# Attention with the pass for the maxima of all 64 items in front of the second pass

## The reference

```python
q = x @ Wq.T + bq; k = x @ Wk.T + bk; v = x @ Wv.T + bv   # then heads, a rotary factor
k = jnp.repeat(k, rep, axis=1); v = jnp.repeat(v, rep, axis=1)
att = jnp.einsum('bhqd,bhkd->bhqk', q, k) / scale
att = jnp.where(causal[None, None], att, -jnp.inf)
att = jax.nn.softmax(att, axis=-1)
y = jnp.einsum('bhqt,bhtd->bhqd', att, v)
return y.transpose(0, 2, 1, 3).reshape(b, t, n) @ Wo.T + bo
```

## Time and profile before

| | us |
|---|---|
| median of 3 runs | 3045.74 |
| lowest and highest | 3042.68, 3046.11 |
| profiled execution | 3042.04 |
| its span | 3040.3 |
| second block of attention, first to last product | 156.09 to 315.8 |
| first product of the third block | 317.40 |

### The profile page before, as it was taken

One profiled execution on the slowest core, in us unless ns is written; L12 is line 12 of the kernel. 1 busy time (PEld: TensorE's weight loads), 2 busy tenths in 40 slices (PEclk: granted clock), 3 DMA queues, 4 the chain that ended last, 5 costly groups with the idle time before them and its releaser, 6 DMA issues. The chain is left out here.

```text
span 3040.3 us, 79963 instructions
## 1 busy us (share of the span) xinstructions
PE 2766.1 (91%) x33106; PEld 2176.6 (72%) x33106; DVE 1597.8 (53%) x3536; ACT 1285.3 (42%) x2840; POOL 469.5 (15%) x603
## 2 busy tenths in 40 slices
PE   7899888999928999999999999999999999699998
PEld 4433557999815777777777777777777778589997
DVE  4444447666424554555555555555554554476763
ACT  1123212223114555655555565556555555332321
POOL 0011000000001222222222222222222322100000
PEclk9979899999958999999999999999999999899999
DMA  1100011111010000000000000000000000111100
GB/s 43 29 1 1 22 49 56 56 35 48 0 28 23 20 16 12 20 23 5 23 20 16 13 20 23 6 23 20 16 12 20 23 6 6 30 56 55 55 28 14
DMA packets 62021, 73.90 MB, mean 24 GB/s; under 512 B 17152, under 2 KB 51344, under 8 KB 61712
## 3 DMA queue, kind: packets, MB, share of 16 engines
q1 hardware_dynamic: 61712, 69.44, 7.5%
HBM read 68.25 MB, written 1.18 MB: 23 GB/s over the span
## 5 line engine op out<-in xcount | busy, mean ns | idle before, releaser
L433 ACT ACTIVATE g_h<-g_ps,g_b_now 128x512 f32<-128x512 f32 x256 | 175.0, 689 | 338.2 <-PE g_ps L457 332.4
L1472 PE MATMUL dn_ps<-dn_zi,dn_wt 64*64 64x64 f32 x5120 | 253.9, 221 | 56.4 <-DVE dn_zi L1818 55.1
L470 PE MATMUL g_ps<-g_w_high,g_h_low 128*128 128x256 f32 x1024 | 289.8, 283 | 0.0
L470 PE MATMUL g_ps<-g_w_low,g_h_high 128*128 128x256 f32 x1024 | 289.8, 283 | 0.0
L470 PE MATMUL g_ps<-g_w_high,g_h_high 128*128 128x256 f32 x1024 | 289.7, 283 | 0.0
L1818 DVE TENSOR_TENSOR dn_zi<-dn_ps,dn_mz 128x128 f32<-128x128 f32 x640 | 162.8, 286 | 232.4 <-PE dn_ps L1462 229.2
L1472 PEld LDWEIGHTS dn_ps<-dn_zi,dn_wt 64*64 64x64 f32 x5120 | 207.3, 135 | 91.8 <-DVE dn_zi L1818 68.6
L1390 PE MATMUL dn_ps<-xnT,dn_w 128*128 128x512 f32 x512 | 251.4, 616 | 22.7 <-DMA dn_w<-in_W_qkvz_dram 14.9
L1721 POOL TENSOR_TENSOR dn_o<-dn_o,dn_zt 128x256 f32<-128x256 f32 x128 | 107.7, 842 | 963.9 <-DVE dn_o L1845 710.5
L1765 DVE SCALAR_TENSOR_TENSOR dn_cv<-dn_raw,dn_cw,dn_cv 128x1024 f32<-128x1024 f32 x192 | 250.3, 1304 | 2.0
L1560 ACT ACTIVATE dn_wt<-dn_ps 128x256 f32<-128x256 f32 x512 | 187.2, 395 | 100.3 <-PE dn_ps L1476 89.3
(11 more groups left out here) (265 smaller groups left out, 5469.7 us busy)
## 6 DMA issues: line engine op xcount, KB each, us to landing
g_w<-in_fc_dram SPq DMA_DIRECT2D x32, 1024.0 KB, 6.5
dn_w<-in_W_qkvz_dram SPq DMA_DIRECT2D x16, 768.0 KB, 4.4
dn_cum_row<-dn_cum_rows SPq DMA_DIRECT2D x32, 256.0 KB, 3.8
dn_wout<-in_W_out_dram SPq DMA_DIRECT2D x16, 256.0 KB, 2.6
f_gate<-in_gateT_dram SPq DMA_DIRECT2D x16, 128.0 KB, 2.1
f_up<-in_upT_dram SPq DMA_DIRECT2D x16, 128.0 KB, 2.3
f_down<-in_downT_dram SPq DMA_DIRECT2D x16, 128.0 KB, 2.4
x_res<-in_x_dram SPq DMA_DIRECT2D x1, 1024.0 KB, 5.2
```

Source lines behind the costliest of these rows:

```text
L433: nc.scalar.activation(h[:, f % 4], h_b[f % 4], ACT.Gelu, bias=b1_now[u // 2][:, f:f + 1]).then_inc(h_ready, 1)
L470: last = pe.matmul(y_b[q % 2][:, 0:D], hidden[:, f, q * P:(q + 1) * P], weights[:, f, :], start=(f == 0 and n == 0), stop=(f == NF - 1 and ...
L1472: mm = pe.matmul(block_of(bD[s], 1, b, h), wt[s][half(h), 1, b, :], zi[s][half(h), b, :], start=True, stop=True)
```

## The change

AHEAD becomes ITEMS. All 64 row items and their maxima come first, then 64 steps with keys and values only. For that, `neg_max` gets one buffer for each of the eight pairs instead of two, and GpSimd clears eight. The functions that place items in the three slots are as before and give 0 to 63 for rows and 64 to 127 for keys.

```diff
 HEADS = REP * B
 ITEMS = HEADS * 2 * HT
-AHEAD = 10
+AHEAD = ITEMS
...
-            neg_max = [sb2(f"neg_max{s}", [P, HT, HKV, SLOT]) for s in range(2)]
+            neg_max = [sb2(f"neg_max{s}", [P, HT, HKV, SLOT]) for s in range(HEADS)]
...
-                        mm = pe.transpose(aux[:, t * P:(t + 1) * P], neg_max[pair % 2][:, t].rearrange("p g s -> p (g s)"), m.ident[:])
+                        mm = pe.transpose(aux[:, t * P:(t + 1) * P], neg_max[pair][:, t].rearrange("p g s -> p (g s)"), m.ident[:])
...
-                for s in range(2):
+                for s in range(HEADS):
                     nc.gpsimd.memset(neg_max[s][:], 0.0).then_inc(zeroed, 1)
...
-                    nc.vector.tensor_reduce(neg_max[pair % 2][:, t, 2 * gp:2 * gp + 2, HD], slot(rows_place(n))[:, :, 0:(t + 1) * P],
+                    nc.vector.tensor_reduce(neg_max[pair][:, t, 2 * gp:2 * gp + 2, HD], slot(rows_place(n))[:, :, 0:(t + 1) * P],
...
-                dve.wait_ge(zeroed, 2)
+                dve.wait_ge(zeroed, HEADS)
```

## The result

The changed kernel takes 3103.76 us (median of 4 runs, 3102.79 to 3111.11) against 3044.79 (4 runs, 3042.68 to 3046.11): 1.020 times as long, 95% interval 1.0182 to 1.0217. Forecast were 3105 us, 3096 to 3122. The profiled execution took 3104.3 us. The second block of attention, first product to first product of the third block, went from 161.3 to 223.6 us, 62.3 more; forecast were 63.3.

What follows compares the result with a forecast made beforehand. TensorE bounds the kernel, at the clock it has. Block: 108.3 + 0.3 + 2.3 + 102.0 + 8.0 + 3.7 = 224.6 us against 161.3, so 3042.0 + 63.3 = 3105.3 us; range 3096 to 3122.

Steps and rivals of the forecast that it cites:

- first pass: All row items with their masks on TensorE: sixteen groups of four at 6.77 us, 108.3 us if the clock stays low.
- clearing: Eight clearings instead of two delay the first maximum by 2.6 us; cost 0.3 us, bounds 0 and 2.6.
- handover: Between the passes, from the end of the last mask to the first keys item: 2.3 us, now 1.80.
- second pass, turns and copies, with its half clock: Keys and values alone with turns and open copies of y: 102.0 us at full clock, plus 8.0 for half clock.
- The low clock: TensorE stays at 0.50 (1.2 GHz) throughout the row items; 13.5 groups cost 39 us more by the clock.
- rival A: The clock rises early in the first pass: block 172.0 us, 10.7 more than now, 3053 us in all; chance 5%.
- Row items at full clock, 3.9 us: Four row items with masks at full clock, summed from pieces, kept for the rival: 3.9 us a group.
- The parting, 1.4 us a group: Four steps take 9.5 us apart against 8.1 mixed, so 1.4 us a group lost; 19 us over 13.5 groups.
- The copy, 0.59 us a pair: In the second pass values wait for ScalarE's copy of y: 0.59 us a pair, open seven times, 4.1 us.
- Half clock in the second pass, 16 us: The second pass begins at 1.2 GHz for 16 us, costing 8 us; the rise comes after 9 to about 40 us.
- B: The clock doesn't rise in the second pass, or not for most of it: block 301 us, 3182 us; chance 5%.
- C: At full clock VectorE sets the first pass at 52.3 us: block 156.2, 5.1 less than now, 3037 us; chance 2%.

Runs made afterwards that it cites:

- the burst: The changed kernel with 64 full-height products added ahead of the first row item: 3069.29 us against 3047.06 for the kernel before, ratio 1.0078.
- the run with two bursts: The changed kernel with 64 products ahead of the first row item and 64 ahead of the first keys item: 3057.04 us against 3044.13, ratio 1.0044.
- 10 ahead: The kernel before, which has 10 row items ahead, with 64 products added ahead of the first: 3038.56 us against 3043.02 without them.
- 12, 16 and 64 ahead: Kernel before at 12 or 16 row items ahead, with 64 products ahead of them: 3031.57 and 3054.39 us; changed kernel with those products: 3069.29.
- 13 ahead: Kernel before with 13 row items ahead instead of 10: 3037.98 us against 3043.02; with 64 products ahead of them also, 3023.43.
- 34 ahead: Kernel before with 34 row items ahead instead of 10, and eight buffers for the maxima: 3072.46 us against 3047.06, ratio 1.009.

## Why the prediction was right, point by point

| term | forecast | measured |
|---|---|---|
| first pass | 108.3 | 108.4 (264.74 + 0.32 - 156.70) |
| clearing | 0.3 | 0 |
| handover | 2.3 | 2.1 (to 267.14) |
| second pass, turns and copies, with its half clock | 110.0 | 109.5 (to 376.62) |
| end | 3.7 | 3.65 |
| block | 224.6 | 223.6 |

- **TensorE as the bound:** right. In the first pass it is busy without a gap, and VectorE waits for it.
- **The low clock:** right as a reading of the earlier trace rows, and the largest term. That a stretch of the kernel before had shown just this work at just this level for 16 us is what made the forecast safe. But the prediction took the level as one of the row items, and they run at either (108.3 us at 0.50, 61.2 at 1.00). It was right because the change left what stands ahead of them as it was: in both kernels the clock is up until the 1.99 us of idle ahead of the block. The rule that sustained matmul activity releases the clock (TensorE: Matmul & The Clock Gate, "What's actually happening", in the Trainium skill) would have given rival A's 3053; the trace after has 108 us of it without a release.
- **Row items at full clock, 3.9 us:** 3.82, by the burst. So 13.5 x (6.77 - 3.82) = 40 us are the clock on the moved items, and one added burst of 5.2 us took 37.5 off the block.
- **The parting, 1.4 us a group:** 1.21. The 8.1 us of four mixed steps took off too much for the turn (0.5 to 0.6 instead of 0.45); it is 8.21. And the reason I gave was mostly wrong. I pointed to the keys and rows that start together; they are 0.42, a third. The other 0.79 goes with the changes of tile shape, which I named only in a sentence aside.
- **The copy, 0.59 us a pair:** right, seen seven times.
- **Half clock in the second pass, 16 us:** 19.0, at a cost of 8.2 us where 8.0 were forecast (109.5 against the 101.3 of the run with two bursts). That it came so close is in part luck: in the burst run, the same pass took 30.6 us to rise. The bounds of 9 to 40 were right to be wide, and the scatter of the times (3102.79 to 3111.11) may be of that kind, but only one execution is profiled.
- **Rivals:** A and B are ruled out by the clock in the profile. C needed a row item under 0.83 us; at full clock it is 3.82 / 4 = 0.96, so not even a full clock would have made VectorE the bound.

## What to carry to other kernels

Before moving work from a mix into a stretch of its own, look for a stretch of the profile that already has that work alone, and read two things there: what a unit costs, and which clock it has. Read the clock at the entry of a stretch, too. Here a pass of products on a part of the rows never lifted TensorE's clock and yet held it, and 5.2 us of dense full-height products ahead of it took 37.5 us off the block; ahead of the kernel before, where less stands to be gained, they took off 3. Filling the idle stretch at the handover took off another 11. Where two passes over small tiles are mixed, the distance between them is a free parameter: 13 instead of 10 changed, within a group, only which strips and sizes meet, and gave 0.66 us of 8.21. Before calling an overlap on TensorE partial, look at when the slot of the late product came free.

## What I had not expected of the hardware

- The clock has a memory here: the same row items, TensorE busy throughout, ran 108 us at 0.50 or 61 us at 1.00, according to what came just before.
- It fell at or behind short idle stretches: at the 1.99 us ahead of the block in all fourteen traces, and at or within 2 us behind the handovers with 0.98 us of idle (10 ahead) and 1.56 us (12, 16 and 64 ahead), but not at one with 1.25 us (13 ahead). With so few cases I can't say whether the idle time or what stands on either side decides.
- Dose matters, and not simply: eight full-height products behind each row item (0.85 us each time) didn't lift the clock in 152 us, 64 in a row did within 3.0 to 3.7 us.
- The mix at 16 ahead, busy without a gap and with values in it, stayed at 0.50 for 58 us in the one execution profiled; the mixes at 10, 12, 13 and 34 ahead rose 9 to 18 us after their first keys item.
- Products in different strips overlap wholly where nothing else holds them: 512 and 256 columns take 1.06 us, as long as the 512 alone. A change of tile shape shows as 0.10 us on either side of it.
